# A linear-attention layer inside a graph-network kernel: key and query steps in pairs

## The chip, the core and the metric

The kernel runs on one core of a Trainium2 chip. The metric is the device time of one execution in microseconds (us). A core has a matrix engine (TensorE, PE in the profile), three engines for elementwise work (VectorE or DVE, ScalarE or ACT, GpSimd or POOL), a queue that mostly issues transfers (SyncE, SP) and 16 DMA engines. Each engine runs its own instructions in order; they wait for each other through semaphores: `wait_ge(sem, n)` holds an engine until the semaphore has reached n, `then_inc(sem, 1)` raises it when an instruction is done. TensorE writes only to PSUM, which has eight banks of 512 numbers in each partition.

## What is computed

The program is a layer of a graph network (four blocks of sparse attention and a small MLP), beside it a Performer layer with linear attention, and behind both a mixture of experts. The change touches the Performer's attention alone. For 1250 nodes, 8 heads of 64 and 256 features:

```python
def softmax_kernel(x, pmat):
    xp = jnp.einsum('bhnd,df->bhnf', x, pmat)
    xp = xp - jnp.max(xp, axis=-1, keepdims=True)
    return jnp.exp(xp) / math.sqrt(pmat.shape[-1])
...
q_prime = softmax_kernel(q, Pmat)
k_prime = softmax_kernel(k, Pmat)
kv = jnp.einsum('bhnf,bhne->bhfe', k_prime, v)
k_sum = jnp.sum(k_prime, axis=2) + 1e-06
z = 1.0 / jnp.einsum('bhnf,bhf->bhn', q_prime, k_sum)[..., None]
attn = jnp.einsum('bhnf,bhfe->bhne', q_prime, kv) * z
attn = attn.transpose(0, 2, 1, 3).reshape(b, n, HEADS * DH)
x = x + attn @ Wproj + bproj
```

## The kernel before

The nodes lie in NT = 10 tiles of P = 125. The 8 heads form G = 4 groups of two (e = 0, 1), which use the two halves of the partitions. A step n is one group and two tiles (b = 0, 1), so there are K_STEPS = 20 key steps (five per group) and Q_STEPS = 20 query steps.

**A key step.** `key_features(n)` lets TensorE multiply the keys by the projection matrix: four products with 64 rows each, into one of three pairs of banks. `key_highest(n)` takes the highest feature of each row (VectorE, one reduction over 1024 numbers). `key_exp(n)` takes four exponentials (ScalarE) into a ring of four. GpSimd adds the two tiles of each head (`attention_pool`), VectorE adds that to the group's sum (`add`). TensorE multiplies values by features into a bank that collects a whole group: four products into a 64-column half each; in the code before they stand in the loop of `attention_pe`, and in this text they are "the value products". At a group's end VectorE copies the bank away (`values_copied`) and TensorE sums the features over the nodes (`key_sums`, bank 7), which `sums_copied` reads. The value products of every group use bank 6, so those of the next group wait for `values_copied`. `turn_sums(g)` transposes a group's values for the query steps.

**A query step.** `query_features(n)` (four products, bank pair n % 2), `highest(n)` (VectorE), `query_exp(n)` (ScalarE, four), then `turn_features(n)`: eight transposes, four per head, into banks 4 and 5. ScalarE copies each half to `qf_cols` (line 2548). `attend(n)` has two parts: eight products with 32 columns for the denominators, then four with 64 columns for the values, all into bank 6 + n % 2. `den_turned(n)` takes the reciprocal (VectorE, line 2498). `spread` copies it by DMA over the partitions of its head: SP issues the two transfers of head 0, GpSimd those of head 1, each of 31.2 KB. `divide(n)` (line 2449) multiplies the values by what has landed, and frees the bank for step n + 2: `attend(n)` waits for `out_made` >= n - 1.

**The order** is written by hand. A round of the query loop on TensorE is features(n), turn(n - 1), attend(n - 2); on VectorE den_turned(n - 3), divide(n - 4), highest(n). On ScalarE a round copies the turned features of step n - 1 and then takes the exponentials of step n. In its first five steps SP issues two loads of rows of x (250 KB each, from `xn_dram`) behind each spread; all its transfers are in one queue. GpSimd adds a bias row to one tile of x ahead of the spread in each of the steps 8 to 17, once all ten tiles have come. Behind the last round stand projections (`project_pe`, four products of 512 columns each), with what is left of the turns and attends between them.

In the program's order and in the profile, all DMA issues have line 118, since one helper issues them; they are told apart by their tiles: `rows<-rows` is a spread, `xbuf<-xn_scratch` a load of x.

## Time and profile before

| | us |
|---|---|
| three runs, lowest / median / highest | 2315.02 / 2317.23 / 2320.78 |
| the profiled execution | 2316.9 |
| its span on the core | 2315.2 |
| TensorE busy in the span | 2288.2 (99%) |
| key steps, 168.44 to 223.82 | 55.4 |
| query steps 2 to 19, 223.82 to 294.02 | 70.2 |
| the end of the query steps, 294.02 to the third projection at 305.06 | 11.0 |

The profile is one execution, and its times count from the start of the span. A timeline row gives start and duration; behind a row, in brackets, is how long its engine idled before it and what ended that. `x8` merges eight instructions (a product of 32-bit numbers counts as two, a transpose as one). The end of a matrix product is modelled, so from one group of products to the next the difference of the starts is the better measure. PEld rows are weight loads, which lie beside the products.

### The profile page before, as it was taken

To read this page: it belongs to the slowest core of one execution; us is meant where nothing else is said; L and a number is where in the kernel's file an instruction comes from. 1 tells how busy PE (TensorE), PEld (TensorE's weight loads), DVE (VectorE), ACT (ScalarE), POOL (GpSimd) and SP (SyncE) were. 2 spreads that over 40 slices of the span, in tenths; PEclk is the share of its full clock that TensorE was granted. 3 is DMA by queue.
4 is the path that set the end of the run, shared out by engine and by line. 5 is a ranking of instruction groups with operands and counts; after the bars stand their busy time and mean duration, and the time that the engine had idled before them with its cause. 6 is when DMAs were issued, how large, how long until landed. Compare 5 with 4: busy or idle time off the path is not lost. (4 is left out here: it accounts for less than half of the span.)

```text
span 2315.2 us, 29925 instructions
## 1 busy us (share of the span) xinstructions
PE 2288.2 (99%) x10169; PEld 1512.6 (65%) x10169; DVE 1431.0 (62%) x2532; ACT 977.1 (42%) x1694; POOL 1276.9 (55%) x1731
## 2 busy tenths in 40 slices
PE   8999999999999999999999999999999999999998
PEld 4565645457677777777877777777767776544443
DVE  8777661524876763777674587676477766634345
ACT  5436642222765331566331376432266633312221
POOL 2004413041666881566894366796266677627776
PEclk9999999999999999999999999999999999999999
DMA  6410211420666310476210176510066621679517
GB/s 185 140 36 6 78 52 42 120 86 1 163 166 176 114 60 1 101 173 159 90 45 23 37 174 162 149 45 24 1 150 169 159 81 32 230 240 348 194 46 242
DMA packets 136882, 260.39 MB, mean 112 GB/s; under 512 B 53564, under 2 KB 55980, under 8 KB 134390
## 3 DMA queue, kind: packets, MB, share of 16 engines
q1 hardware_dynamic: 88520, 152.11, 22.4%
q0 software_dynamic: 46864, 104.03, 16.2%
q10 hardware_dynamic: 1346, 2.33, 0.3%
q8 instruction: 82, 1.34, 0.2%
q14 instruction: 70, 0.57, 0.1%
HBM read 213.17 MB, written 32.20 MB: 106 GB/s over the span
## 5 line engine op out<-in xcount | busy, mean ns | idle before, releaser
L118 POOL DMA_DIRECT2D cols<-w x720 | 353.3, 499 | 220.3 <-PE psum L1074 174.1
L1074 PE MATMUL psum<-cols,rows 125*128 125x256 f32 x1600 | 368.4, 379 | 0.0
L1061 PE MATMUL psum<-g_k_cols,g_q_cols 128*125 128x512 f32 (+1 forms) x960 | 360.8, 513 | 0.2
L1074 PEld LDWEIGHTS psum<-cols,rows 125*128 125x128 f32 x1600 | 303.1, 190 | 36.5 <-DMA cols<-w 0.3
L1156 DVE CUSTOM_DVE_ANT_0 g_prob<-psum,ln_count 125x1250 f32<-125x1250 f32 x160 | 233.9, 1462 | 102.8 <-PE psum L1061 102.5
L1061 PEld LDWEIGHTS psum<-g_k_cols,g_q_cols 128*125 128x125 f32 x960 | 179.4, 187 | 165.2 <-issue 155.5
L1254 ACT ACTIVATE g_prob<-g_prob,g_row_max 125x1250 f32<-125x1250 f32 x160 | 215.8, 1349 | 125.0 <-DVE g_row_max L1156 123.1
L1170 DVE STREAM_TRANSPOSE w<-g_prob 128x1280 f32<-128x1280 f32 x160 | 241.5, 1509 | 34.2 <-DMA cols<-w 24.9
L1260 ACT ACTIVATE g_prob<-g_prob,g_row_max 125x1250 f32<-125x1250 f32 x160 | 215.5, 1347 | 67.3 <-DVE g_row_max L1145 67.1
L580 POOL TENSOR_TENSOR rows<-rows,g_bias_rows 125x512 f32<-125x512 f32 x40 | 50.0, 1270 | 186.1 <-DVE rows L570 186.1
L3436 PE MATMUL psum<-m_ew,m_x_cols 128*64 128x256 f32 (+1 forms) x576 | 150.2, 493 | 0.0
L3535 DVE TENSOR_TENSOR m_work<-psum,m_eb 128x768 f32<-128x768 f32 x27 | 40.8, 1511 | 124.2 <-PE psum L3436 124.1
L412 PE MATMUL psum<-cols,w 128*128 128x375 f32 (+1 forms) x416 | 115.2, 426 | 0.0
L2152 DVE TENSOR_TENSOR p_shared<-iota,p_shared 125x1024 f16<-125x1024 f16 x100 | 91.8, 968 | 27.0 <-PE psum L2166 25.8
L412 PE MATMUL psum<-rows,w 128*128 128x375 f32 (+1 forms) x368 | 101.0, 425 | 0.0
L412 PEld LDWEIGHTS psum<-cols,w 128*128 128x128 f32 x416 | 77.7, 189 | 30.3 <-ACT g_k_cols L430 0.9
L916 POOL TENSOR_TENSOR xbuf<-xbuf,g_prob 125x256 f32<-125x256 f32 x120 | 87.2, 727 | 11.5
L3436 PEld LDWEIGHTS psum<-m_ew,m_x_cols 128*64 128x64 f32 x576 | 58.1, 138 | 52.9 <-issue 45.0
L412 PEld LDWEIGHTS psum<-rows,w 128*128 128x128 f32 x368 | 68.7, 188 | 26.8
L3593 POOL DMA_INDIRECT m_ew<-in_L_ffn_expert_w,m_weights_of x64 | 65.5, 1024 | 29.1 <-issue 18.0
L893 DVE TENSOR_TENSOR xbuf<-xbuf,psum 125x256 f32<-125x256 f32 x80 | 33.7, 421 | 75.3 <-PE psum L748 35.3
L462 DVE TENSOR_TENSOR g_k_cols<-g_k_cols,psum 128x375 f32<-128x375 f32 (+1 forms) x32 | 15.4, 480 | 102.9 <-PE psum L412 102.8
(460 smaller groups left out, 4572.4 us busy)
## 6 DMA issues: line engine op xcount, KB each, us to landing
cols<-w POOLq DMA_DIRECT2D x720, 80.0 KB, 3.2
cols<-w SPq DMA_DIRECT2D x560, 80.0 KB, 3.5
w<-in_L_gnn_m_w SPq DMA_DIRECT2D x8, 1024.0 KB
slot_rows<-p_kf SPq DMA_DIRECT2D x1, 7344.0 KB, 33.4
rows<-slot_rows SPq DMA_DIRECT2D x54, 136.0 KB, 7.3
m_ew<-in_L_ffn_expert_w SPq DMA_DIRECT2D x4, 1536.0 KB, 9.5
xbuf<-xn_scratch SPq DMA_DIRECT2D x20, 250.0 KB
slot_outputs<-slot_rows SPq DMA_DIRECT2D x1, 5000.0 KB
```

The source lines that it names most:

```text
L118: return eng.dma_start(out, in_, allow_slow_non_contiguous=True)
L412: ins = pe.matmul(c.bank(SEVEN_BANKS[p][u], width).rearrange("p (j n) -> p j n", n=P), left, right, start=(k == 0 and p in (1, 5, 6, 7)), ...
L916: g.tensor_tensor(pair_x(j, 1, 1), pair_x(j, 1, 1), pair_part(of, j, 1 + i), ALU.add).then_inc(of.pool_made, 1)
L1061: ins = pe.matmul(psum[0:P, at:at + width], q_cols[:, h, t * P:(t + 1) * P], k_cols[:, h, start:start + width], start=True, stop=True)
L1074: ins = pe.matmul(c.bank(6 + g % 2, 256).rearrange("p (u a i) -> p u a i", u=2, a=SIDE), rows[0:P, j, h * 128:(h + 1) * 128], turned_keys[ ...
L1156: v.tensor_tensor_reduce(prob_keys[u], by_tile(psum[0:P, at:at + N]), by_tile(ln_count[:, t, :]), -SCORE_SCALE, -NOT_AN_EDGE / 10, ALU.add ...
L1170: v.transpose(square[s][:, :, u, :].rearrange("p b (j i) -> p b j i", i=SQUARE), prob_squares[u]).then_inc(squared, 1)
L1254: s.activation(prob_keys[u], prob_keys[u], ACT.Exp, bias=row_max[:, u, 0:1], scale=-1.0, accum_out=row_max[:, u, 2:3]).then_inc(exp_made, 1)
L1260: s.activation(prob_keys[u], prob_keys[u], ACT.Identity, scale=row_max[:, u, 3:4]).then_inc(prob_made, 1)
L2152: v.tensor_tensor(hots[:, b % 2, :, c0:c0 + width].rearrange("p k (j c) -> p k j c", c=SAME), iota[:, 0:width].rearrange("p (j c) -> p j c ...
L3436: ins = pe.matmul(psum[lanes(e), at:at + cn], x_cols[i % 2][:, k, lanes(e)], ew1[s][:, k, c0:c0 + cn], start=(k == 0), stop=(k == KC - 1))
L3593: g.indirect_dma_start(out=into[s].rearrange("p c o -> p (c o)"), out_offset=None, in_=from_, in_offset=bass.IndirectOffsetOnAxis(ap=weigh ...
```

## The change

The key steps run in pairs on TensorE: features n and n + 1, then the value products of n - 2 and n - 1. The groups use bank 6 and 7 in turn (`group_bank`), for the value products and for the key sums. VectorE takes two maxima in a row, then the two adds. The first query features stand directly behind the last key features.

The query steps run in pairs too: turn(n - 2), features n and n + 1, turn(n - 1), then both denominators, then both values. For that `attend` is split, and `turn_features` waits for each half's copy instead of both. VectorE takes two reciprocals, a maximum, two divisions, a maximum. ScalarE copies both turned steps and then takes eight exponentials. SP loads one tile of x behind each of the first ten spreads. GpSimd adds the bias rows behind the spreads: two behind each of the spreads 10 and 11, one behind each of 12 to 17 (`bias_behind`).

```diff
+        def bias_behind(n):
+            per_step = [0] * NT + [2, 2] + [1] * (NT - 4)
+            return range(sum(per_step[:n]), sum(per_step[:n + 1]))
...
                 spread(sp, n, 0)
-                for t in range(2 * n, min(2 * n + 2, NT)):
-                    load(sp, x[:, t, :], xn_dram[t * P:(t + 1) * P, :]).then_inc(res_in, 16)
+                if n < NT:
+                    load(sp, x[:, n, :], xn_dram[n * P:(n + 1) * P, :]).then_inc(res_in, 16)
...
+        def group_bank(g):
+            return 6 + g % 2
...
+            values(0)
+            for n in range(3, K_STEPS, 2):
+                key_features(n)
+                if n + 1 < K_STEPS:
+                    key_features(n + 1)
+                else:
+                    query_features(0)
+                values(n - 2)
+                values(n - 1)
+                for g in range(G):
+                    if NT // 2 * (g + 1) - 1 in (n - 5, n - 4):
+                        key_sums(g)
+            turn_sums(0)
+            turn_sums(1)
+            query_features(1)
+            values(K_STEPS - 1)
+            turn_sums(2)
...
             def turn_features(n):
                 pe.wait_ge(qf_made, 4 * (n + 1))
-                pe.wait_ge(*((qf_cols_made, 2 * n) if n else (kv_cols_made, G - 1)))
                 for e in range(2):
+                    pe.wait_ge(*((qf_cols_made, 2 * n - 1 + e) if n else (kv_cols_made, G - 1)))
...
-            for n in range(2, Q_STEPS):
+            for n in range(2, Q_STEPS, 2):
+                turn_features(n - 2)
+                if n == 2:
+                    turn_sums(G - 1)
+                    key_sums(G - 1)
                 query_features(n)
+                query_features(n + 1)
                 turn_features(n - 1)
+                denominators(n - 2)
+                denominators(n - 1)
                 attend(n - 2)
+                attend(n - 1)
             pe.wait_ge(w_in[2], 16)
             pe.wait_ge(qf_made, 4 * (Q_STEPS - 1))
             project_pe(0)
+            turn_features(Q_STEPS - 2)
             turn_features(Q_STEPS - 1)
             project_pe(1)
+            denominators(Q_STEPS - 2)
+            denominators(Q_STEPS - 1)
             attend(Q_STEPS - 2)
             attend(Q_STEPS - 1)
...
-            for n in range(2, Q_STEPS):
-                if n >= 3:
-                    den_turned(n - 3)
+            for n in range(2, Q_STEPS, 2):
+                if n >= 4:
+                    invert(n - 4)
+                    invert(n - 3)
+                highest(n)
                 if n >= 4:
                     divide(n - 4)
-                highest(n)
+                    divide(n - 3)
+                highest(n + 1)
...
             for n in range(Q_STEPS):
-                t = n - (Q_STEPS - NT) + 2
-                if 0 <= t < NT:
+                spread(g, n, 1)
+                if n == NT:
                     g.wait_ge(res_in, 16 * NT)
+                for t in bias_behind(n):
                     g.tensor_tensor(x[:, t, :], x[:, t, :], bias_rows[:, 1, :], ALU.add).then_inc(bp_added, 1)
-                spread(g, n, 1)
```

Where instructions go is best seen in the program's order. TensorE in the query steps before (p_pmat and p_q_cols: features; ident and p_kf: a turn; 32 columns: denominators; 64: values):

```order
L2281 MATMUL psum<-p_pmat,p_q_cols 125x256 x4
L2383 MATMUL psum<-ident,p_kf 128x125 x8
L2400 MATMUL psum<-p_shared 32x125 x8
L2405 MATMUL psum<-p_shared 64x250 x4
L2281 MATMUL psum<-p_pmat,p_q_cols 125x256 x4
L2383 MATMUL psum<-ident,p_kf 128x125 x8
L2400 MATMUL psum<-p_shared 32x125 x8
L2405 MATMUL psum<-p_shared 64x250 x4
```

and in the changed kernel, the same amount of work:

```order
L2285 MATMUL psum<-p_pmat,p_q_cols 125x256 x8
L2396 MATMUL psum<-ident,p_kf 128x125 x8
L2413 MATMUL psum<-p_shared 32x125 x16
L2422 MATMUL psum<-p_shared 64x250 x8
L2396 MATMUL psum<-ident,p_kf 128x125 x8
```

Two steps had eight groups of products of unlike shape; now they have five, and the second step's denominators stand right behind the first's.

SP in the first query steps, before:

```order
L118 DMA rows<-rows 64x1x125 x2
L118 DMA xbuf<-xn_scratch 125x512 x2
L118 DMA rows<-rows 64x1x125 x2
L118 DMA xbuf<-xn_scratch 125x512 x2
L118 DMA rows<-rows 64x1x125 x2
```

and in the changed kernel, where the four rows of a pair are issued one behind the other:

```order
L118 DMA rows<-rows 64x1x125 x2
L118 DMA xbuf<-xn_scratch 125x512
L118 DMA rows<-rows 64x1x125 x2
L118 DMA xbuf<-xn_scratch 125x512
L118 DMA rows<-rows 64x1x125 x2
```

A load now stands between the spreads of the same pair; half as many bytes go with each spread, over twice as many spreads.

GpSimd in the query steps of the changed kernel (before, the run of spreads was 16 rows long, and single adds stood between the later ones):

```order
L118 DMA rows<-rows 64x1x125 x22
L2904 TENSOR_TENSOR xbuf<-xbuf,p_bias_rows 125x512 x2
L118 DMA rows<-rows 64x1x125 x2
L2904 TENSOR_TENSOR xbuf<-xbuf,p_bias_rows 125x512 x2
L118 DMA rows<-rows 64x1x125 x2
```

Two adds now stand between spread 10 and spread 11, whose reciprocals are neighbours.

## Rows read from the trace of the kernel before

**Rows 1.** The stretches: us, busy us (instructions) of each engine, TensorE clock, DMA share, GB/s
```profile
168.44:223.82 55.38, 50.66 (x393) 31.34 (x393) 43.51 (x45) 36.58 (x95) 27.24 (x24) 1.00 0.07 22
...
235.90:257.00 21.10, 17.82 (x196) 11.26 (x194) 11.53 (x14) 12.12 (x29) 5.22 (x10) 1.00 0.39 131
```

**Rows 2.** TensorE in the key steps, in order of time: start, us, engine, line, operation
```profile
168.44 2.86 PE L2281 MATMUL psum<-p_pmat,rows 64*125 64x256 f32 x24
...
172.66 1.08 PE L2365 MATMUL psum<-p_kf,xbuf 125*64 125x256 f32 x8 [0.39 <-ACT p_kf L2253]
...
200.36 1.10 PE L2333 MATMUL psum<-p_ones,p_edge_sum 125*128 125x64 f32 x8
201.39 1.13 PE L2281 MATMUL psum<-p_pmat,rows 64*125 64x256 f32 x8
202.46 1.08 PE L2365 MATMUL psum<-p_kf,xbuf 125*64 125x256 f32 x8
...
209.85 1.08 PE L2365 MATMUL psum<-cols,xbuf 125*64 125x256 f32 x8 [1.10 <-DVE p_shared L2457]
...
216.05 0.66 PE L2349 MATMUL psum<-ident,p_shared 128*128 128x128 f32 x4
...
223.82 1.13 PE L2281 MATMUL psum<-p_pmat,p_q_cols 64*125 64x256 f32 x8
```

**Rows 3.** VectorE and ScalarE in a key step, in order of time
```profile
204.65 1.23 DVE L2261 TENSOR_REDUCE p_mx<-psum 125x4 f32<-125x1024 f32 x1
...
205.91 1.57 ACT L2253 ACTIVATE cols<-psum,p_mx 125x256 f32<-125x256 f32 x4 [0.51 <-DVE p_mx L2261]
```

**Rows 4.** VectorE's add of the key sums (line 2474): ns min/median/max
```profile
L2474 DVE TENSOR_TENSOR p_edge_sum<-p_edge_sum,cols x16: 681/1014/1508, 178.1 to 222.0; 125x512 f32<-125x512 f32 x16
```

**Rows 5.** A query step before the long waits, in order of time
```profile
227.45 1.13 PE L2281 MATMUL psum<-p_pmat,p_q_cols 64*125 64x256 f32 x8
227.57 0.95 DVE L2498 RECIPROCAL rows<-psum 128x125 f32<-128x125 f32 x1 [1.34 <-PE psum L2405]
...
228.51 1.07 PE L2383 MATMUL psum<-ident,p_kf 125*128 125x125 f32 x8
...
229.25 1.05 ACT L2548 COPY p_shared<-psum 128x500 f32<-128x500 f32 x2 [1.16 <-PE psum L2383]
...
229.51 0.64 PE L2400 MATMUL psum<-p_shared 128*32 128x125 f32 x16
...
230.08 1.07 PE L2405 MATMUL psum<-p_shared 128*64 128x250 f32 x8
...
231.07 1.13 PE L2281 MATMUL psum<-p_pmat,p_q_cols 64*125 64x256 f32 x8
```

**Rows 6.** From a reciprocal to its division while rows of x arrive
```profile
239.43 0.94 DVE L2498 RECIPROCAL rows<-psum 128x125 f32<-128x125 f32 x1 [0.60 <-PE psum L2405]
240.40 1.19 SPq L118 DMA_DIRECT2D rows<-rows  x2
...
241.63 0.87 SPq L118 DMA_DIRECT2D xbuf<-xn_scratch  x2
...
246.10 0.42 DVE L2449 TENSOR_TENSOR cols<-psum,rows 128x250 f32<-128x250 f32 x1 [1.38 <-DMA rows<-rows]
```

**Rows 7.** Landing of the spreads issued near 241, near 258.5 and near 284 us
```profile
DMA to landing us min/median/max: 2.2/4.7/5.1
...
DMA to landing us min/median/max: 1.8/1.9/2.2
...
DMA to landing us min/median/max: 2.2/3.1/3.9
```

**Rows 8.** GpSimd between two spreads
```profile
263.09 1.31 POOL L2862 TENSOR_TENSOR xbuf<-xbuf,p_bias_rows 125x512 f32<-125x512 f32 x1
```

**Rows 9.** TensorE at the end of the query steps
```profile
294.02 3.70 PE L2430 MATMUL psum<-w,cols 128*125 128x512 f32 x8
...
305.06 3.70 PE L2430 MATMUL psum<-w,cols 128*125 128x512 f32 x8
```

More of the change, by code:

```diff
@@ L2332, in key_sums @@
                     at = (2 * half + e) * DH
-                    ins = pe.matmul(c.bank(7, 4 * DH)[:, at:at + DH], group_sum[:, g % 2, e, half * 128:(half + 1) * 128],
+                    ins = pe.matmul(c.bank(group_bank(g), 4 * DH)[:, at:at + DH], group_sum[:, g % 2, e, half * 128:(half + 1) * 128],
                                     ones[:], start=True, stop=True)
@@ new lines, in values @@
+            def values(m):
+                g, u = divmod(m, NT // 2)
+                pe.wait_ge(kf_made, 4 * (m + 1))
+                if u == 0 and g == 1:
+                    pe.wait_ge(counted, BLOCKS)
+                if u == 0 and g >= 2:
+                    pe.wait_ge(ks_made, g - 1)
+                for b in range(2):
+                    for e in range(2):
+                        ins = pe.matmul(c.bank(group_bank(g), F)[e * DH:(e + 1) * DH], values_of(2 * u + b, 2 * g + e),
+                                        key_slots(m)[:, 2 * e + b, :], start=(u == 0 and b == 0),
+                                        stop=(u == NT // 2 - 1 and b == 1))
+                ins.then_inc(kv_mm, 1)
@@ L2385, in turn_features, with denominators @@
                     ins.then_inc(qf_turned, 1)
-            def attend(n):
+            def denominators(n):
                 g = n // (NT // 2)
@@ L2474, in add, with invert @@
                 v.tensor_tensor(group_sum[:, g % 2], group_sum[:, g % 2], step_sum[:, n % 4], ALU.add).then_inc(kf_added, 1)
-            for n in range(2, K_STEPS + A_LAG):
-                if n < K_STEPS:
-                    key_highest(n)
-                elif n < K_STEPS + 2:
-                    highest(n - K_STEPS)
-                if n >= A_LAG and (n - A_LAG) % (NT // 2) >= 1:
-                    add(n - A_LAG)
-                g, u = divmod(n - K_LAG + 1, NT // 2)
-                if u == 0 and 1 <= g <= G:
-                    values_copied(g - 1)
-                g, u = divmod(n - A_LAG - 1, NT // 2)
-                if u == 0 and 1 <= g:
-                    sums_copied(g - 1)
+            key_highest(2)
+            for n in range(3, K_STEPS, 2):
+                for g in range(G):
+                    if NT // 2 * (g + 1) - 1 in (n - 4, n - 3):
+                        values_copied(g)
+                    if NT // 2 * (g + 1) - 1 in (n - 7, n - 6):
+                        sums_copied(g)
+                key_highest(n)
+                if n + 1 < K_STEPS:
+                    key_highest(n + 1)
+                else:
+                    highest(0)
+                for m in (n - 3, n - 2):
+                    if m % (NT // 2) >= 1:
+                        add(m)
+            sums_copied(G - 2)
+            add(K_STEPS - 2)
+            highest(1)
+            values_copied(G - 1)
+            add(K_STEPS - 1)
             sums_copied(G - 1)
-            def den_turned(n):
+            def invert(n):
                 v.wait_ge(out_mm, n + 1)
@@ L2510, in attention_dve @@
             project_dve(1)
[L2511 to L2512 removed]
+            invert(Q_STEPS - 2)
+            invert(Q_STEPS - 1)
             v.wait_ge(qf_turned, 2 * Q_STEPS)
@@ L2538, in query_exp, with copy_features @@
                                  bias=mx[:, 4 * (n % 2) + i:4 * (n % 2) + i + 1]).then_inc(qf_made, 1)
+            def copy_features(n):
+                if n >= 2:
+                    s.wait_ge(out_mm, n - 1)
+                for e in range(2):
+                    s.wait_ge(qf_turned, 2 * n + 1 + e)
+                    s.copy(qf_cols[:, n % 2, e], qf_turned_out(e)).then_inc(qf_cols_made, 1)
             query_exp(0)
@@ L2542, in attention_act @@
             query_exp(1)
-            for n in range(1, Q_STEPS + 1):
-                if n >= 3:
-                    s.wait_ge(out_mm, n - 2)
-                for e in range(2):
-                    s.wait_ge(qf_turned, 2 * n - 1 + e)
-                    s.copy(qf_cols[:, (n - 1) % 2, e], qf_turned_out(e)).then_inc(qf_cols_made, 1)
-                if n == 1:
+            for n in range(2, Q_STEPS + 1, 2):
+                copy_features(n - 2)
+                if n == 2:
                     copy_sums(G - 1)
-                if 2 <= n < Q_STEPS:
+                copy_features(n - 1)
+                if n < Q_STEPS:
                     query_exp(n)
+                    query_exp(n + 1)
         beyond_sems = range(beyond_ends.num, beyond_added.num + 1)
```

51 lines of the change are left out of this document (12 added, 39 removed).

## The prediction

> **What bounds the kernel now.** I read the stretches first. TensorE is busy 99% of the span, but not evenly: in the key steps it works 50.66 of 55.38 us, and in the query steps from 235.90 to 257.00 it works 17.82 of 21.10 [rows 1]. Its clock is at the upper level (2.4 GHz) in both. Then I read the timeline at TensorE's gaps. In the key steps the value products of a new group wait for VectorE's copy of the old group's bank, 1.10 us [rows 2]; there are three such places. In the slow query stretch TensorE waits for `divide`, which waits for a spread: the reciprocal of 239.43 ends at 240.37, its division starts at 246.10, 5.73 us later [rows 6]. Outside that stretch a step costs 3.62 us (227.45 to 231.07) and consists of TensorE's work alone [rows 5].
>
> **What a change of shape costs.** Three features in a row take 2.86 us, one takes 1.13: the second and third cost 0.87 each. Features with value products behind them cost 1.07 (201.39 to 202.46) [rows 2]. So a change of shape costs about 0.2 us, and I take 0.19 for every kind. That is an estimate for transposes, denominators and values, of which no row shows two groups side by side.
>
> **Key steps.** Before, a pair costs 2 x 2.07 = 4.14: features 1.07 and values 1.00 each (I take the 1.00 of the query steps' values, 230.08 to 231.07) [rows 2, 5]. After: 0.87 + 1.07 + 0.81 + 1.00 = 3.75. From the first value products to the third query features the new order is one group of values (1.00), nine pairs (33.8), three key sums of 1.03 (200.36 to 201.39, 3.1), and then the old ending from 216.05 to 223.82 (7.77) less one features and one values group that now stand in the pairs (2.07), 5.7 [rows 2]. Sum 43.6. Before it took 51.2 (172.66 to 223.82, same rows). If TensorE never waited, 7.6 us would go; the three waits at the bank are part of that.
>
> It will wait some. VectorE has five maxima (1.23 each) [rows 3], four adds (1.01 each, 0.68 to 1.51 as they meet GpSimd's work) [rows 4] and two small copies (0.4 each, an estimate from the division's 0.42 [rows 6]) per group: 11.0 us at most, against TensorE's 2.5 x 3.75 + 1.03 = 10.4. They are nearly even, and in four groups VectorE may be late by up to 2.4. And the first query features stand directly behind the last key features, while they need the exponentials of key step 18, whose features were issued a pair before. From the start of that earlier pair: maximum of 17 at 1.2, of 18 to 3.5, exponentials of 17 to 4.0 and of 18 to 5.6 (1.57 each) [rows 3]. TensorE is there at 3.75 + 0.87 = 4.6 and waits 1.0. With another 1.1 for late maxima the gain is **5.5 us** (4.5 to 7.6).
>
> **Query steps, TensorE's own work.** Before, the starts are 1.06, 1.00, 0.57 and 1.00 apart [rows 5], 7.26 for two steps. After, a round is turn 1.00, features 0.87 + 1.06, turn 1.00, denominators 0.38 + 0.57, values 0.81 + 1.00: 6.69. But a wait is added in the middle. The second step's denominators need ScalarE's two copies of its turn, which before had a whole step to arrive. The copies start 0.74 after the turn and take 1.05 [rows 5], so they end at 1.79, and TensorE wants them at 1.00 + 0.38. That costs 0.45, with both values and the next turn queued behind it: 7.15 a round. The copies take back most of what the shapes give.
>
> **Query steps, the loop through the spread.** A bank is used again two steps later, so values, reciprocal, spread, division and denominators form a loop. Before it could take 7.24 us: values, 1.12 to the reciprocal's start (0.12 behind the next features) [rows 5], 0.94, spread, 0.47 for the division and its signal, 0.57 for denominators. That left 4.15 for the spread; while x arrives it takes 5.73 [rows 6], and (1.12 + 0.94 + 5.73 + 0.47 + 0.57) / 2 = 4.4 is the slow step. After, time counts from the first turn of a round. The two reciprocals run from -0.7 to 0.25 and from 0.25 to 1.2. SP issues four transfers and one load in line: first spread 0.3 to 1.45, load to 1.9, second spread 1.9 to 3.1 (1.19 a spread, 0.43 a load) [rows 6], its last transfer from 2.5. The second spread is what decides: its division must be ready 2.38 us before the round can end (0.57 denominators, 0.81 and 1.00 values).
>
> Without a load the last transfer goes at 2.0, lands 2.2 later if all is clear and 3.9 later if not [rows 7], is divided by 4.7 or 6.4, and the round takes 7.15 or 8.8. With a load I take 5.1 less half: the slow landing of 5.1 us had two loads and more ahead in the same queue, the clear one 1.9 to 2.2 [rows 7]. Half of the excess of 2.9 gives 3.7, from 2.5 to 6.2, round 9.0; the whole excess gives 7.6 and a round of 10.4, none gives 4.7 and 7.5. DMA shares point to the upper half: in the slow stretch the share is 0.39 for a transfer rate of 131 GB/s [rows 1], so a load of 250 KB takes some 2 us of its engines by itself. I take **9.2** for the five rounds with loads (steps 4 to 12), 8.4 to 10.0.
>
> The Trainium skill ("DMA: Bandwidth & Descriptors", anatomy of one DMA) fits a transfer as 2.0 us and its bytes at 436 GB/s, with no term for what lies ahead in the queue. By it a spread lands in 2.1 us whatever stands before, and the loads would cost this round nothing but SP's 0.43 us; the landing of 5.1 us in this trace contradicts it. The same page says (queues, rings and completion order) that on each DMA engine descriptors are consumed in ring order, which is what the late landings behind x look like, and which speaks against a load between the two spreads of a pair.
>
> GpSimd's half has a cover that goes. Before, an add (1.31) [rows 8] stood ahead of a spread and ran while TensorE worked. After, two stand between spreads 10 and 11: first spread 0.5 to 1.55, adds to 4.2, second spread's last transfer 4.75, landed 6.7, divided 7.1, round 9.5. In the last two rounds it is one add: landed at 5.4 to 5.7, round 8.3.
>
> Rounds: 7.15 less the turn that lies before (6.15), 5 x 9.2, 9.5, 2 x 8.3 = 78.3 us, against 70.2 from 223.82 to 294.02. **8.1 us are lost** (2 to 12).
>
> **The end.** Two projections with what stands between took 11.04 [rows 9]. Now both last turns stand between them, the second half-waiting for a copy (2.3 instead of 0.85), and the attends save 0.4: plus 1.1. Behind the third projection the order is the same and TensorE was busy without a gap, so I let the difference reach the end whole.
>
> **Sum**: -5.5 + 8.1 + 1.1 = +3.7 on the profiled execution's 2316.9, which is 0.3 under the median of the runs: **2321.0**.
>
> **Rivals.**
> - *The single loads do no harm* (the rule of the page above would give this). The five rounds take 7.3; the sum is 6.15 + 36.5 + 9.5 + 16.6 = 68.8, and with -5.5 and +1.1 the kernel is at 2311, or 2306 if GpSimd's adds do no harm either. For it: half as many bytes per spread, and the queue is empty when a round starts. Against it: spread two is issued right behind a load. Chance 0.18; it is faster by over 0.3% (7 us) in 0.11.
> - *Slower outright*: the second spread waits for the whole load. From a landing 5 us after the last issue on, a round costs 10; the loads' rounds then cost 50, late landings [rows 7] hit the others too, and with a key gain of 4.5 the kernel ends near 2327. Chance 0.17, of which 0.15 beyond 0.3%.
> - *VectorE is the bound in the key steps*: adds at 1.5 make a group 12.1 us, the key gain shrinks to 2, and the kernel is at 2324.5. For it: adds now come in twos while GpSimd works. Against it: the median of 1.01. Chance 0.08, half of it slower.
> - *The change in the middle doesn't reach the end*, since a weight load or the next stage's transfers end last: 2317. Chance 0.05.
> - My forecast, 2317 to 2324, has 0.52, of which 0.04 slower by over 0.3%.
>
> So faster 0.11, same 0.66, slower 0.23; 0.3% is about what a measurement of this kernel can tell. The range of 2311 to 2327 leaves out the lower half of the first rival and the upper half of the second.
>
> **What would show it.** In the changed profile: key steps in rounds of 3.75 to 4.2 with no wait for the bank's copy; the third query features near 218; in the query steps the wait of TensorE in front of the second denominators, put down to ScalarE's copy in the first round and to `divide` in the later ones; rounds of 9.2 while x arrives, one of 9.5 with GpSimd's two adds, then 8.3; the third projection near 309. I am wrong if rounds with loads are near 7.3, if denominators wait for nothing, or if VectorE's maxima end each round of the key steps.

## The result and the profile after

The changed kernel takes 2328.0 us (median; 2326.5 to 2330.7) against 2317.2 us (2315.0 to 2320.8). The ratio is 1.0045 with a 95% interval of 1.0035 to 1.0055, 10.8 us more; the prediction had 2321.0 and at most 2327. The profiled execution took 2330.7 us, its span 2328.9. Ratios leave out executions that were far slower than all others of their kernel (2990 us once below, 4884 us once for the kernel before).

The stretches of the changed kernel's trace, in the columns of [rows 1]: the key steps, the query steps to the first projection, one round with loads, and two short windows in the query steps:

```profile
171.89:222.54 50.65, 47.69 (x394) 32.40 (x393) 42.29 (x45) 35.45 (x95) 28.59 (x24) 1.00 0.07 25
222.54:307.44 84.90, 67.15 (x714) 46.29 (x713) 42.89 (x52) 45.34 (x108) 27.02 (x40) 0.92 0.20 56
236.76:241.29 4.53, 4.53 (x33) 2.30 (x33) 2.02 (x2) 1.57 (x4) 0.32 (x1) 0.50 0.05 16
277.83:282.36 4.53, 4.53 (x33) 2.30 (x33) 2.02 (x2) 1.57 (x4) 0.32 (x1) 0.50 0.03 12
250.57:260.38 9.81, 6.97 (x82) 4.92 (x81) 4.88 (x7) 5.14 (x13) 2.09 (x4) 1.00 0.26 80
```

The key steps fell from 55.38 [rows 1] to 50.65 us. The query steps rose from 70.20 (223.82 to 294.02) to 84.90. TensorE's work there isn't the cause: in the round of 9.81 us it is busy for 6.97. And in both windows of 4.53 us its granted clock is 0.50, the lower of its two levels (1.2 GHz), which the trace of before never shows in these stages. The whole stretches at that level are longer, 6.8 us each: 235.7 to 242.5 and 276.6 to 283.4. They begin while TensorE still waits.

TensorE in the key steps, in order of time, which answers to [rows 2]:

```profile
177.12 2.00 PE L2285 MATMUL psum<-p_pmat,rows 64*125 64x256 f32 x16
179.04 1.08 PE L2367 MATMUL psum<-p_kf,xbuf 125*64 125x256 f32 x8
179.96 1.03 PE L2367 MATMUL psum<-cols,xbuf 125*64 125x256 f32 x8
180.92 2.00 PE L2285 MATMUL psum<-p_pmat,rows 64*125 64x256 f32 x16
...
210.15 1.13 PE L2285 MATMUL psum<-p_pmat,rows 64*125 64x256 f32 x8
213.02 1.13 PE L2285 MATMUL psum<-p_pmat,p_q_cols 64*125 64x256 f32 x8 [1.74 <-ACT cols L2257]
```

A pair takes 3.80 us (177.12 to 180.92) and the waits for the bank's copy are gone. The first query features wait 1.74 us for the exponentials.

One round of the query steps while x arrives, in order of time; it answers to [rows 5, 6]:

```profile
250.57 1.07 PE L2396 MATMUL psum<-ident,p_kf 125*128 125x125 f32 x8
250.81 1.18 SPq L118 DMA_DIRECT2D rows<-rows  x2
...
252.03 0.48 SPq L118 DMA_DIRECT2D xbuf<-xn_scratch  x1
252.56 1.68 SPq L118 DMA_DIRECT2D rows<-rows  x2
...
253.89 0.41 DVE L2474 TENSOR_TENSOR cols<-psum,rows 128x250 f32<-128x250 f32 x1
...
254.50 0.64 PE L2413 MATMUL psum<-p_shared 128*32 128x125 f32 x16
257.50 0.42 DVE L2474 TENSOR_TENSOR cols<-psum,rows 128x250 f32<-128x250 f32 x1 [3.20 <-DMA rows<-rows]
...
257.97 0.63 PE L2413 MATMUL psum<-p_shared 128*32 128x125 f32 x16 [2.84 <-DVE cols L2474]
258.54 1.91 PE L2422 MATMUL psum<-p_shared 128*64 128x250 f32 x16
```

The landing of SP's half of this round's first spread (issued from 250.8) and of its second (from 252.6), then of GpSimd's half of both (from 251.1), in the form of [rows 7]:

```profile
DMA to landing us min/median/max: 1.9/2.2/2.5
...
DMA to landing us min/median/max: 3.0/3.6/4.3
...
DMA to landing us min/median/max: 1.8/2.1/4.5
```

On SP the spread ahead of the load lands in 2.5 us at most, the one behind it in 4.3. GpSimd issues its four transfers in a queue of its own, without a load in it, and the last of them, issued at 252.6, half a microsecond behind SP's load, lands in 4.5 us. In the other four rounds with loads the last transfer lands in 4.3 to 4.8 us on SP's queue and in 4.3 to 4.7 on GpSimd's, while the transfer right behind the load on SP's queue takes 2.4 to 2.6. So late is the last transfer of each half, on either queue, and not simply what stands behind the load in its queue. The division waits 3.20 us for both halves, the second denominators wait 2.84 for the division, and both steps' values stand behind them. The rounds that begin at 228.75, 241.29, 250.57, 260.38 and 270.17 take 12.54, 9.28, 9.81, 9.79 and 12.19 us. Then come 8.90 and twice 8.1.

TensorE around the second fall of the clock:

```profile
277.83 1.06 PE L2413 MATMUL psum<-p_shared 128*32 128x125 f32 x16 [3.10 <-DVE cols L2474]
278.82 3.60 PE L2422 MATMUL psum<-p_shared 128*64 128x250 f32 x16
282.36 1.59 PE L2396 MATMUL psum<-ident,p_kf 125*128 125x125 f32 x8
```

Behind the wait of 3.10 us the values start 0.99 us after the denominators instead of 0.57, and take 3.54 instead of 1.84. Denominators and values together come 2.1 us late, with the next turn 2.6. The end of the stage answers to [rows 9]:

```profile
307.44 3.70 PE L2455 MATMUL psum<-w,cols 128*125 128x512 f32 x8
...
319.62 3.70 PE L2455 MATMUL psum<-w,cols 128*125 128x512 f32 x8
```

That is 12.18 us between the first and the third projection, against 11.04.

One trap when the two traces are laid side by side: in this execution the key steps began at 171.89, in that of before at 168.44. That difference of 3.45 us arose ahead of all changed code. In the other traces of this study, with the same code ahead of them, the first key features stand between 169.4 and 176.3 and don't go with what was changed behind them. I therefore compare lengths of stages inside a trace, and medians for the whole.

### The profile page after: what moved, and what is told of

It is laid out like the page before. It is cut to its first block and busy times, and to the rows that moved or that the text cites. A ratio compares the mean times of both kernels' runs of the same rounds, so it can differ in the third digit from the quotient of the medians.

```text
span 2328.9 us, 29926 instructions
## 1 busy us (share of the span) xinstructions
PE 2288.3 (98%) x10169; PEld 1520.2 (65%) x10169; DVE 1429.6 (61%) x2532; ACT 974.5 (42%) x1694; POOL 1276.0 (55%) x1731
## 3 DMA queue, kind: packets, MB, share of 16 engines
q8 instruction: 82, 1.34, 0.2%
## 5 line engine op out<-in xcount | busy, mean ns | idle before, releaser
L3634 POOL DMA_INDIRECT m_ew<-in_L_ffn_expert_w,m_weights_of x64 | 65.6, 1025 | 27.4 <-issue 17.4
```

## The experiments

Ratios are to the kernel before on the same chip, with 95% intervals. They are what is compared, since the chips differ by up to 5 us for the kernel before. Differences to the change in us are worked out from the ratios; by the medians some come out up to 4 us otherwise.

### The two halves apart

Key steps of the change, everything behind them as before (TensorE's and SP's part shown; VectorE, ScalarE and GpSimd follow):

```diff
-            for n in range(2, Q_STEPS, 2):
-                turn_features(n - 2)
-                if n == 2:
-                    turn_sums(G - 1)
-                    key_sums(G - 1)
+            turn_features(0)
+            turn_sums(G - 1)
+            key_sums(G - 1)
+            for n in range(2, Q_STEPS):
                 query_features(n)
-                query_features(n + 1)
                 turn_features(n - 1)
-                denominators(n - 2)
-                denominators(n - 1)
                 attend(n - 2)
-                attend(n - 1)
...
-                if n < NT:
-                    load(sp, x[:, n, :], xn_dram[n * P:(n + 1) * P, :]).then_inc(res_in, 16)
+                for t in range(2 * n, min(2 * n + 2, NT)):
+                    load(sp, x[:, t, :], xn_dram[t * P:(t + 1) * P, :]).then_inc(res_in, 16)
```

> The key steps of the change (pairs, groups in two banks, the first query features in the last pair), with the query steps, loads and GpSimd adds as they were before. Theory A (the key steps gain 4.7 us as in the changed kernel's profile, third query features about 4.7 us earlier, and the gain reaches the end whole): 2317.2 - 4.7 = 2312.5 us, ratio 0.998. Theory B (in the changed kernel the work of the key steps began 3.5 us later than before, and that belongs to the change): 2316 us. Theory C (VectorE, now shorter of time, gives the gain back before the query steps): 2317, and the key rounds are above 4.1 us.

Measured: 2312.7 against 2317.5 us, ratio 0.9979 (0.9970 to 0.9987), 4.8 us less. Theory A. The trace shows something new at the first query features:

```profile
210.97 1.13 PE L2285 MATMUL psum<-p_pmat,p_q_cols 64*125 64x256 f32 x8 [1.75 <-ACT cols L2257]
212.03 1.56 PE L2367 MATMUL psum<-p_kf,xbuf 125*64 125x256 f32 x8
213.37 1.92 PE L2367 MATMUL psum<-cols,xbuf 125*64 125x256 f32 x8
```

Value products that take 0.91 and 0.97 in the changed kernel's trace take 1.34 and 1.86: the granted clock was 0.50 from 212.5 to 215.9, and the key steps took 52.30 us (169.82 to 222.12) instead of 50.65. In the changed kernel's trace it didn't fall there.

The other half, the key steps as before and the query steps, loads and adds of the change:

> The key steps as before; the query steps, the single loads of x and the GpSimd adds as in the changed kernel. Theory A (the two parts add up): the query steps lose 14.7 us and the end 1.1, so 2317.2 + 15.8 = 2333.0 us, with rounds of 9.3 to 9.8 us while rows of x arrive and two of about 12.3 in which TensorE's granted clock falls to 0.5. Theory B (the loss hangs on the earlier start of the query steps, because transfers of the stage before are then still under way): 2328 or less, and no round of 12.

Measured: 2336.7 us, ratio 1.0075 (1.0063 to 1.0088), 17.4 us more (19.2 by the medians) where 15.8 were expected. Its query steps took 88.18 us, with a mean clock of 0.90 over them: it fell four times, behind waits of 1.80, 2.01, 2.43 and 4.37 us, and not behind waits of 3.09 and 2.77. The halves give -0.0021 and +0.0075, the sum of +0.0054 is within the intervals of the change's +0.0045. Theory B is refuted: the loss belongs to the query steps.

### What of the loads makes the round long

The bytes of the loads left out, their place in SP's queue kept:

```diff
-                    load(sp, x[:, n, :], xn_dram[n * P:(n + 1) * P, :]).then_inc(res_in, 16)
+                    load(sp, x[:, n, 0:8], xn_dram[n * P:(n + 1) * P, 0:8]).then_inc(res_in, 16)
```

> The changed kernel, but each of the ten loads of x moves 8 columns of a row instead of all, so the rest of x is not the residual: it leaves out nearly all bytes of the loads and keeps their issue in SP's queue. Theory A (the bytes ahead in the queue hold the second spread back): the five rounds with loads take 7.2 to 7.7 us as my rival had it, TensorE's clock doesn't fall, and the kernel ends near 2328.0 - 16 = 2312 us. Theory B (the place in SP's queue costs as much as the bytes): rounds near 8.8 us, about 2322 us. Theory C (the loop is slow for another reason, since it is 8.1 us even without loads): rounds as in the changed kernel, 2328 us.

Measured: 2314.8 us, ratio 0.9993 (0.9983 to 1.0004), 12 us less than the change. The five rounds take 7.58, 7.41, 8.27, 7.41 and 7.41 us, the clock stays up in them:

```profile
226.25:264.33 38.08, 34.93 (x403) 24.62 (x401) 24.53 (x31) 25.58 (x62) 10.62 (x20) 1.00 0.16 36
```

Theory A: without the bytes the rounds are what TensorE's work asks. The issue of a load on SP (some 0.5 us) costs about 0.15 a round (7.41 against the 7.27 of a clear round below).

The loads whole again, but both of a pair issued behind its second spread:

```diff
-                if n < NT:
-                    load(sp, x[:, n, :], xn_dram[n * P:(n + 1) * P, :]).then_inc(res_in, 16)
+                for t in (n - 1, n) if n % 2 == 1 and n < NT else ():
+                    load(sp, x[:, t, :], xn_dram[t * P:(t + 1) * P, :]).then_inc(res_in, 16)
```

> The changed kernel, but both loads of a pair are issued behind the pair's second spread, so that nothing stands between the two spreads in SP's queue; the same bytes in the same five rounds. Theory A (the load ahead of the second spread is what makes it late): rounds with loads 7.4 to 8.1 us, no fall of the clock, 2328.0 - 12 = 2316 us. Theory B (the bytes share the 16 DMA engines with GpSimd's and the next pair's spreads whatever their place): rounds of 9.3 to 10, 2328. In between, if the two loads are still under way when the next pair's first spread is issued: rounds of 8.6, 2322.

Measured: ratio 0.9989 (0.9976 to 1.0002), 13 us less than the change with the same bytes in the same rounds. SP, VectorE and TensorE in one of them:

```profile
240.54 2.48 SPq L118 DMA_DIRECT2D rows<-rows  x4
...
243.06 0.90 SPq L118 DMA_DIRECT2D xbuf<-xn_scratch  x2
...
244.39 0.42 DVE L2474 TENSOR_TENSOR cols<-psum,rows 128x250 f32<-128x250 f32 x1 [0.36 <-DMA rows<-rows]
...
245.16 0.64 PE L2413 MATMUL psum<-p_shared 128*32 128x125 f32 x16 [0.30 <-ACT p_shared L2581]
```

The wait for the spread is down from 3.20 to 0.36 us, and TensorE now waits 0.30 for ScalarE's copy. Such a round takes 7.3 us. The five rounds with loads took 7.37, 7.27, 8.45, 7.27 and 7.27 us; the next one, with GpSimd's two adds between its spreads, took 12.15 with a fall of the clock in it (the 10.0 named in a later expectation is too low), and the last two took 7.9 and 8.1. So what costs is a load issued ahead of a spread that is waited for, and not the same bytes behind it. It does not show that the order within SP's queue is the reason: here the loads stand behind GpSimd's transfers too, and in the change those were as late. What the Trainium skill says ("DMA: Bandwidth & Descriptors", queues, rings and completion order), that descriptors of a ring are taken in its order, fits SP's late spreads and leaves GpSimd's unexplained. The same page's fit of 2.0 us and bytes, which it measured on GpSimd's path, comes near GpSimd's transfers in a clear round (1.8 to 1.9 us) and is far from the 4.3 to 4.7 us of its last one in the change's rounds with loads.

The loads on ScalarE's queue:

```diff
-                if n < NT:
-                    load(sp, x[:, n, :], xn_dram[n * P:(n + 1) * P, :]).then_inc(res_in, 16)
...
+                if n == 4:
+                    s.wait_ge(kv_mm, K_STEPS)
+                    for t in range(NT):
+                        s.wait_ge(xn_out[t], 32)
+                for t in (n - 4, n - 3) if 4 <= n < NT + 4 else ():
+                    load(s, x[:, t, :], xn_dram[t * P:(t + 1) * P, :]).then_inc(res_in, 16)
                 if n < Q_STEPS:
                     query_exp(n)
```

> The changed kernel, but the loads of x are issued by ScalarE behind its copies of a pair, two a round in the same number of rounds, so that SP's queue holds only spreads; they start some 3 us earlier in a round than SP's did, and ScalarE pays for the issue. Theory A (the order within one queue makes the spread late): rounds 7.4 to 8.1, 2316 us. Theory B (the DMA engines themselves are shared, so another queue doesn't help): rounds of 9 to 10, 2326 to 2328. Theory C (ScalarE's issue costs its exponentials, which then end last): rounds above 8.5 with TensorE waiting for the activation instead of the division.

Measured: ratio 0.9996 (0.9983 to 1.0008), not to be told from the loads behind the pair, 11 us less than the change. In the trace these loads start later in the round than SP's did, not earlier: in the round of 251.69 at 255.74, when all its spreads have been issued. So this run doesn't tell queue from time either. Where the loads were fully under way when the next round's spreads were issued (from 235.3; the DMA share just before is 0.33), the first two landed in 2.7 and 3.6 us on SP's queue and in 2.2 and 3.1 on GpSimd's, against 1.8 to 2.2 in the round of 251.69, in whose first microsecond the loads end. A load in a third queue thus costs a spread something too. A run with a load issued between the two spreads, but on a third queue, was not made.

The loads and adds as they were before, with the paired steps:

```diff
-                if n < NT:
-                    load(sp, x[:, n, :], xn_dram[n * P:(n + 1) * P, :]).then_inc(res_in, 16)
+                for t in range(2 * n, min(2 * n + 2, NT)):
+                    load(sp, x[:, t, :], xn_dram[t * P:(t + 1) * P, :]).then_inc(res_in, 16)
...
-                spread(g, n, 1)
-                if n == NT:
+                t = n - (Q_STEPS - NT) + 2
+                if 0 <= t < NT:
                     g.wait_ge(res_in, 16 * NT)
-                for t in bias_behind(n):
                     g.tensor_tensor(x[:, t, :], x[:, t, :], bias_rows[:, 1, :], ALU.add).then_inc(bp_added, 1)
+                spread(g, n, 1)
```

> The changed kernel with the loads of x and GpSimd's adds as before: two loads behind each of the first five spreads, one add ahead of spreads 8 to 17. Theory A (only what stands between the two spreads of a pair delays the round): the first two loads' rounds take 12 us, the third 9.8, the rest 7.6 to 8.1, the clock falls in the first ones; 2323 us. Theory B (each load costs its round 2.4 us wherever it stands): 2328. Theory C (two slow rounds of 14 with clock falls): 2329 or more.

Measured: ratio 1.0043 (1.0028 to 1.0059), equal to the change. From features to features, two rounds take 14.1 and 13.4 us at a mean clock of 0.76 and 0.74, one 11.6, and the rest 7.3 to 8.5, as theory C has it:

```profile
231.44:245.57 14.13, 9.46 (x81) 6.08 (x80) 5.15 (x7) 5.15 (x13) 3.21 (x6) 0.76 0.30 96
...
245.57:258.95 13.38, 9.64 (x81) 6.36 (x80) 4.99 (x6) 5.25 (x13) 2.29 (x5) 0.74 0.31 99
```

My theory A (12, 12 and 9.8) was too low, in good part by what the lower clock takes. Fewer rounds suffer, each of them more: moving to single loads, with GpSimd's adds moved along, neither helped nor hurt the paired steps.

### Single loads in single steps

Here the same move has another effect. The changed key steps, the old query steps, but loads and adds of the change:

> The key steps of the change and the old order of query steps (as in the first experiment, 2312.7 us), but with the change's single loads (one behind each of the first ten spreads) and its GpSimd adds (behind the spread, two each at steps 10 and 11). In the first experiment seven steps while x arrives took 30.1 us where seven undisturbed ones take 25.4, so the loads cost 4.7 us. Theory A (it is the number of loads between two spreads that counts, and one fits into the slack of 4.15 us that a single step leaves its spread): no step above 3.9 us, and 2310 us; GpSimd's two pairs of adds may take back up to 2. Theory B (the bytes cost the same wherever they stand): ten steps of 4.1, 2312.5. Theory C (each spread with a load in its way is as late as with two): 2317.

Measured twice: 0.9952 (0.9935 to 0.9970), and 0.9969 (0.9955 to 0.9982) on another chip (below), some 9 us less than before. From 223.86 to 256.61, nine steps with loads, TensorE is busy for 32.71 of 32.75 us:

```profile
223.86:256.61 32.75, 32.71 (x361) 21.37 (x360) 20.67 (x25) 22.69 (x55) 8.51 (x16) 1.00 0.32 88
```

And with nothing else changed against the kernel before:

> The kernel before with one thing from the change: one load of x behind each of the first ten spreads instead of two behind each of the first five, and GpSimd's adds behind their spreads (two each at steps 10 and 11). Theory A (the seven slow steps of before, 4.7 us, go, whatever the key steps are): 2317.2 - 5 = 2312 us, ratio 0.998. Theory B (it works only with the paired key steps, which let the query steps start at another time): ratio 1.000.

Measured: ratio 0.9983 (0.9973 to 0.9993), 4 us less. Theory A, with the interval's upper end below 1. GpSimd's adds moved too; by the traces they count for little: the eight steps from the third query features on take 29.50 us instead of 33.11, the ten behind them 36.85 instead of 37.09. A step needs its spread only a whole step later, and that slack (4.15 us in the prediction) holds one load. Two it did not hold.

### What of the order on TensorE and GpSimd

The first step's values ahead of the second's denominators:

```diff
                 denominators(n - 2)
-                denominators(n - 1)
                 attend(n - 2)
+                denominators(n - 1)
                 attend(n - 1)
```

> The changed kernel with TensorE's order in a round altered in one point: denominators of the first step, its values, denominators of the second, its values, so that the first step's values no longer stand behind the wait for the second step's division. Loads and adds as in the change. Theory A (what makes the loop long is that both steps' values queue behind the later division, and the first reciprocal and spread with them): loads' rounds fall from 9.8 to about 8.8 us, the waits are shorter and the clock falls less: 2322 us, ratio 1.002. Theory B (the late second spread alone sets the round, whatever TensorE does ahead of it): rounds of 9.8, ratio 1.0045 as the change.

Measured: ratio 1.0005 (0.9995 to 1.0016), 9 us less than the change though it has two more changes of shape a round; the loads' rounds took 8.56, 9.04, 9.16, 10.43 (with a fall of the clock) and 8.22 us. The gain is larger than theory A gave, and theory B is refuted. Queueing both values behind the later division cost far more than the shapes gain.

All of GpSimd's adds behind the pair's second spread, and the loads too, as two of the experiments above had them (that part of the edit isn't repeated):

```diff
-            per_step = [0] * NT + [2, 2] + [1] * (NT - 4)
+            per_step = [0] * NT + [0, 3, 0, 3, 0, 2, 0, 2]
```

> The changed kernel with both loads of a pair and all of GpSimd's adds (3, 3, 2 and 2) behind the pair's second spread, so that on neither queue anything stands between the two spreads of a pair. In the kernel with the loads alone moved, rounds were 7.3 us (one 8.45), then 10.0 with the two adds between and a fall of the clock, and 8.1 in the last two. Theory A (pairing itself costs nothing, all loss is what stands between the spreads): every round 7.3, 4 us less than there, ratio 0.997 to before, near the first experiment's 0.998. Theory B (the last adds end late and hold back the first projection): ratio 0.999. Theory C (the second spread is late even with a clear queue, since the pair leaves it no slack): rounds of 8, ratio 0.9995.

Measured: ratio 0.9974 (0.9965 to 0.9983), theory A. Six of eight full rounds take 7.27 to 7.4 us, the last two among them, which took 8.1 in the change. Such a round:

```profile
235.15:242.42 7.27, 6.97 (x83) 4.95 (x81) 4.89 (x7) 4.93 (x13) 2.10 (x4) 1.00 0.34 105
```

One round of 8.66 remains where GpSimd's second spread of the pair (step 11) stands behind the wait for the last load:

```profile
268.09 1.05 POOL L118 DMA_DIRECT2D rows<-rows  x2 [1.02 <-DMA xbuf<-xn_scratch]
```

Another of 8.55 begins at 242.42; in the kernel with small loads the same round took 8.27, so x isn't its cause. In it the last transfers of the second spread land in 3.5 us (SP) and 3.4 (GpSimd), where its others take 1.8 to 2.2. At 245.4, while they are under way, the trace has one packet of 0.02 MB in a queue called `instruction`. The same stands in the traces of small loads, of loads behind the pair and of the pairs with late first query features: of their five rounds with loads only this one has such a packet 0.2 to 1.1 us behind the issue of its last transfers, and these land in 2.8 to 3.7 us. (Another such packet falls in the round of 8.66.) No experiment moved the packet, so this is a coincidence in four traces, and the cause isn't shown.

### What the falls of the clock cost

Dummy products in the wait of the five rounds with loads:

```diff
                 denominators(n - 2)
+                for _ in range(6 if 2 < n < 14 else 0):
+                    pe.matmul(psum[0:128, 6 * BANK + 3 * P:6 * BANK + 3 * P + 128], ident[:], ident[:], start=True, stop=True)
                 denominators(n - 1)
```

Measured: ratio 1.0041 (1.0028 to 1.0055), not to be told from the change. In the trace the five rounds have no fall:

```profile
228.17:277.98 49.81, 42.62 (x462) 31.70 (x461) 24.53 (x31) 25.80 (x62) 10.61 (x20) 1.00 0.27 78
```

They take 49.8 us instead of 53.6, so by these two executions two falls cost 3.8 there and not the 4.8 by which TensorE's work in them was longer: the transfers go on meanwhile, and the round behind a fall had been shorter (9.28). But the clock fell in the next round and behind the first query features instead, and the median gained nothing. The mean granted clock over the whole span agrees that falls became fewer: 0.998 to 1.000 in the five executions with dummies, 0.996 to 0.998 in the six of the change. So the falls went where TensorE was kept busy, in one trace and, by the mean, in the others; that the kernel gets faster by it is not shown, and 3.8 us is no more than the difference of two executions. The dummies also show the loop without falls: 9.9 to 10.0 us a round.

### The best form of each, and the first query features

Against the kernel with single loads in single steps, the first query features placed late:

```diff
-                else:
-                    query_features(0)
                 values(n - 2)
-                values(n - 1)
+                if n + 1 < K_STEPS:
+                    values(n - 1)
...
             turn_sums(1)
+            query_features(0)
+            values(K_STEPS - 2)
             query_features(1)
...
                 else:
+                    add(n - 3)
                     highest(0)
-                for m in (n - 3, n - 2):
+                for m in (n - 3, n - 2) if n + 1 < K_STEPS else (n - 2,):
```

> The fifth experiment's kernel (paired key steps, single query steps, single loads; 0.995 of before), but the first query features no longer stand in the last pair: the order is the last key features, values, key sums, two turns, the first query features, values. Before the first query features TensorE waited 1.74 us in every profile, and in some of them its clock fell behind that wait, which costs another 1.65. Theory A (the wait is the place's fault): no wait above 0.8 us there, no fall, the third query features 51.2 - 7 = 48 to 50 us behind the first key features instead of 52.3, and 2 to 3.4 us less than the fifth experiment: 0.994 of before. Theory B (ScalarE's exponentials set the time; the wait only moves to the next instruction): 0.995, as the fifth.

Measured: 0.9959 (0.9946 to 0.9973). A wait of 0.29 us remains (before value products), and the key steps took 49.35 us (171.53 to 220.90) instead of 52.30, as theory A has it. But the medians, from different chips, showed no gain. So both ran on one chip, beside the best form of pairing (all loads and adds behind the pair, and the first query features late too):

> The fifth experiment's kernel once more, beside the ninth's on one chip. Theory A (the wait of 1.74 us before the first query features and the fall behind it cost what the profiles show, 52.3 against 49.4 us for the key steps): 0.0013 above the ninth's. Theory B (they cost nothing in the median, since in most executions the clock doesn't fall there and later waits take the rest up): the two ratios are the same within 0.0005.

> The ninth experiment's kernel once more, on the same chip as the fifth's. Theory A: 0.9945 of before, the fifth's at 0.9958. Theory B: both at 0.9955.

> The eleventh experiment's kernel (paired query steps with loads and adds behind the second spread) with the first query features placed late, as in the ninth: the best form of pairing both. Theory A (pairing query steps has no price of its own: a round is 7.27 us, two single steps are 7.26): what is left against single steps is the end, 1.1 us, and the rounds of 8.6 behind two groups of loads or adds, 2.6 us, so 3.7 us or 0.0016 more than the ninth's kernel on the same chip. Theory B (pairing costs more than the trace of one execution shows, by falls of the clock in the other executions): 0.003 more, or worse.

Measured: early 0.9969 (0.9955 to 0.9982), 2309.7 us; late 0.9961 (0.9948 to 0.9974), 2308.5 us; pairs 0.9974 (0.9965 to 0.9983), 2312.9 us. The late place is worth 1.2 us in the medians, which these intervals can't tell from nothing; with 0.0008 between the ratios neither theory is decided. Pairing the query steps in its best form comes out 0.0013 or 3 us behind single steps (4.4 by the medians), near the 3.7 of theory A; the intervals overlap, so this is likely and not proven. The late form in single steps beats both kernels of this case: 2308.5 against 2318.4 us.

## Why the prediction was wrong

**Key steps** (forecast 5.5, 4.5 to 7.6): right within its range. 4.7 in the trace and 4.8 in the medians. The pair took 3.80 (3.75 forecast). VectorE was late by 0.3 us, where 1.1 was allowed; the first query features waited 1.74 us, where it was 1.0.

**TensorE's own work in a round** (6.69, with the copy's wait 7.15): mis-sized in both terms, with little harm. The work is 6.97 (for two steps it was 7.26). Features save what I forecast (two take 1.93), values 0.16 instead of 0.19. The denominators save nothing in a round, since a wait stands between their two groups; behind the second projection, where they do stand side by side (316.79 to 317.78), two take 0.99 instead of 1.14. The copy's wait is 0.30 instead of 0.45, so the sum is 7.27.

**The loop through the spread** (9.2 a round with loads, 8.4 to 10.0): this is the term that failed. The loop was right, with the load between two spreads, the later landing and both values queued behind it. The landing was mis-sized: the 3.7 us that I chose were 4.3 to 4.8, and the undisturbed rounds took 9.8 us, or 9.9 to 10.0 where dummies kept the clock up, five times 0.7 us more than forecast. That is the rival "slower outright" (a round of 10, 2327 us), to which I gave 0.17. The row at hand, a landing of 5.1 us with two loads ahead [rows 7], bore its price as well as mine. I took half of the excess for half of the bytes; it was nearer three quarters. The reason I gave was wrong in part as well. I put the late landing down to what stands ahead in SP's queue, and worked out SP's half of the spread alone. The last transfer of GpSimd's half, in a queue without loads, took 4.3 to 4.7 us as well: in the round shown it landed at 257.1, and SP's at 257.4. With SP's queue clear, the division would have waited almost as long. How the load holds both back isn't shown.

**The clock**, a term that was missing. I read that the clock was at the upper level and priced waits by their length alone. Two of the new waits, of 1.84 and 3.10 us, run over into work at 1.2 GHz (4.53 us of it and the next turn), and the rounds with them take 12.4 instead of 9.8. Part of it comes back in the next round. Forecast for the five rounds were 46.0 us, measured 53.6; by the comparison of the two traces some 3.8 of the 7.6 are the clock and the rest the landings. Since the median with dummies was no lower, what the clock costs the whole kernel stays open.

**GpSimd's adds** (9.5, then 8.3 twice): 8.90, 8.08 and 8.10. The order was right, and with the adds behind the pair the last rounds fell to 7.3. One wait I had overlooked: GpSimd waits for all loads behind spread 10, ahead of spread 11.

**The end** (+1.1): +1.14.

**The change reaches the end whole**: -4.7, +14.7 and +1.1 make 11.1, the medians say 10.8. The rival that it doesn't was wrong, as were the rivals of harmless single loads (in pairs; in single steps they are a gain, and the small loads' rounds of 7.4 to 8.3 us show what that rival needed) and of VectorE as the bound.

The interplay was what I had not weighed. Single loads gain 4 us in single steps and nothing in pairs, and pairing costs little with clear queues and some 20 us without (1.0045 against 0.9952 and 0.9969). I read this from the order of the program: a single step gives its spread a whole further step to land, while a pair needs both of its buffers, and so both spreads, within the same round.

## What to carry over

Before steps are paired to save changes of shape (0.3 us a pair here), count what is issued between the two transfers that the pair needs, on any queue and not only on theirs: one load there cost 2.5 us a round, behind the pair it cost next to nothing. Issue what must not wait ahead of what may, on the DMA queue as on the engine. And price a new wait of TensorE (here they were 1.7 us and more) with what follows it, too: it may be followed by some microseconds at half the clock, in some executions and not in others.

## What the hardware showed that I had not expected

- The granted clock fell to 0.50 for 6.8 us, from within waits of 1.84 and 3.10 us to well behind them. With waits of 2.84 us here and of 3.09 in the kernel with only the query steps changed it did not fall, so the length of a wait alone doesn't tell. The wait of 1.74 us ahead of the first query features was followed by a fall in some traces and not in others, with the same code up to there. The Trainium skill ("TensorE: Matmul & The Clock Gate", Part 1) says that the clock follows how busy TensorE has just been; the falls behind waits, and their absence with dummy products in the wait, agree.
- The small transfers of a spread (31.2 KB each) land in 1.8 to 2.4 us with loads issued behind them. With one load of 250 KB issued ahead of them the last one lands in 4.3 to 4.8 us on the load's queue and in 4.3 to 4.7 on GpSimd's, which holds no load.
- A packet of 0.02 MB in the `instruction` queue fell together with spreads that landed 0.9 to 1.8 us late, on both queues, in four traces.
- ScalarE could issue two loads a round (0.26 to 0.36 us for each) without TensorE waiting for its exponentials.
